# Z projections in front of the running places, and state products grouped by form, in a fused embed, state-space and experts kernel

## The reference

```python
h = concatenate([tok(A, B, x, log_dt), softmax(table)[x_txt]], axis=1)     # 16 x 192 x 512
zxbcdt = layernorm(h) @ W_in.T                      # z 1024, x 1024, B 64, C 64, dt 16
xBC = silu(causal_conv4(xBC)); dt = softplus(dt + dt_bias)
state = state * exp(dt * A) + dt * B * x            # per head (16 heads of 64 channels)
y = state . C + D * x                               # for every token
y = rmsnorm(y * silu(z)) * norm_w
h = h + y @ W_out.T
h = h + experts(layernorm(h))                       # router: top 8 of 32 experts, rerouted by similarity
```

## Time and profile before

| | |
|---|---|
| median of 3 runs | 1762.59 us (1762.48 to 1763.11) |
| profiled execution, its own time | 1780.81 us |
| its span in the trace | 1779.1 us |
| mean granted TensorE clock | 0.917 of full |
| TensorE matmul busy | 1574.6 us, 89% |
| VectorE busy | 971.2 us, 55% |
| ScalarE busy | 730.3 us, 41% |
| GpSimd busy | 781.5 us, 44% |
| matmuls of line 1213 (state products, main) | 512 records, 84.7 us |
| matmuls of line 1216 (state products, tail) | 512 records, 49.0 us |

### The profile page before, as it was taken

How to read it: one execution, slowest core, us unless ns; L and a number is a source line. 1 busy time by engine, 2 the same in 40 slices (tenths; PEclk the granted TensorE clock), 3 DMA queues, 4 the chain that set the end, 5 groups by cost and what they waited for, 6 DMA issues and landing times. The chain is left out here.

```text
span 1779.1 us, 31373 instructions
## 1 busy us (share of the span) xinstructions
PE 1574.6 (89%) x9263; PEld 1146.1 (64%) x9264; DVE 971.2 (55%) x2325; ACT 730.3 (41%) x1592; POOL 781.5 (44%) x638
## 2 busy tenths in 40 slices
PE   7999999997599999999999670099999999999996
PEld 7999999975477576675766340066655666666564
DVE  5555554523768998889789545034333343433443
ACT  2525253522776765857658100033333333333332
POOL 4230300011042357677675567545544555555554
PEclk9999999988799998998899575599999999999999
DMA  7210000003355352443423110167767777777665
GB/s 267 77 60 1 13 1 13 1 18 134 114 152 143 93 153 77 134 130 93 151 64 90 27 37 2 60 181 190 159 154 188 162 181 167 169 183 182 162 114 92
DMA packets 97703, 195.20 MB, mean 110 GB/s; under 512 B 38391, under 2 KB 46879, under 8 KB 92880
## 3 DMA queue, kind: packets, MB, share of 16 engines
q0 software_dynamic: 36992, 88.26, 23.1%
q1 hardware_dynamic: 60624, 105.78, 19.5%
HBM read 144.15 MB, written 49.84 MB: 109 GB/s over the span
## 5 line engine op out<-in xcount | busy, mean ns | idle before, releaser
L1888 PE MATMUL moe_ps_gu<-moe_wgu,moe_xt 128*128 x960 | 331.9, 489 | 0.0
L1746 POOL DMA_INDIRECT out_h<-moe_yy,moe_idx_s x121 | 190.9, 1578 | 256.2 <-DVE moe_idx_s L1808 117.4
L1016 POOL DMA_INDIRECT scratch_slots<-lay_toki,lay_slot x192 | 219.9, 1145 | 59.0 <-issue 58.1
L1888 PEld LDWEIGHTS moe_ps_gu<-moe_wgu,moe_xt 128*128 128x128 f32 x960 | 173.7, 191 | 96.6 <-issue 1.2
L1785 ACT ACTIVATE moe_sl<-moe_ps_gu 128x192 f32<-128x192 f32 x120 | 39.7, 331 | 365.7 <-PE moe_ps_gu L1888 336.2
L1411 DVE SCALAR_TENSOR_TENSOR lay_xa<-lay_ring,head_cw,lay_xa 128x378 f32<-128x378 f32 (+5 forms) x240 | 141.9, 609 | 54.4 <-ACT lay_xa L1068 46.0
L1197 PE MATMUL lay_ring<-lay_xnt,win_sb 128*128 128x128 f32 (+2 forms) x1152 | 167.6, 292 | 4.3 <-DVE lay_xa L1411 2.0
L1281 PE MATMUL lay_ring<-head_wout,lay_yb 128*128 128x512 f32 x384 | 170.1, 597 | 0.0
L1197 PEld LDWEIGHTS lay_ring<-lay_xnt,win_sb 128*128 128x128 f32 (+2 forms) x1152 | 150.6, 200 | 10.5 <-issue 3.8
L1740 POOL DMA_INDIRECT moe_xg<-scratch_xg,moe_idx_g x123 | 131.4, 1069 | 47.5 <-issue 28.7
L247 POOL TENSOR_TENSOR tok_vv<-tok_w 128x512 f32<-128x512 f32 x16 | 16.6, 1040 | 259.7 <-ACT tok_w L449 225.5
(11 more groups left out here) (290 smaller groups left out, 2961.5 us busy)
## 6 DMA issues: line engine op xcount, KB each, us to landing
lay_m<-scratch_cum SPq DMA_DIRECT2D x16, 1536.0 KB
moe_wgu<-in_wgu SPq DMA_DIRECT2D x32, 768.0 KB
moe_wd<-in_wd SPq DMA_DIRECT2D x32, 384.0 KB
out_h<-lay_hres SPq DMA_DIRECT2D x48, 128.0 KB
scratch_xg<-lay_x SPq DMA_DIRECT2D x48, 128.0 KB
win_sb<-in_win SPq DMA_DIRECT2D x1, 4384.0 KB, 16.3
tok_u_raw<-in_tok_u SPq DMA_DIRECT2D x16, 256.0 KB, 4.5
tok_v_raw<-in_tok_v SPq DMA_DIRECT2D x16, 256.0 KB, 5.1
```

The costliest lines, as they stand in the source:

```text
L1016: pool.indirect_dma_start(out=a["slots"], out_offset=bass.IndirectOffsetOnAxis(ap=slot[:, j, k:k + 1], axis=0), in_=toki[:, j:j + 1], in_o ...
L1746: pool.indirect_dma_start(out=a["out"], out_offset=bass.IndirectOffsetOnAxis(ap=idx_s[n][:, 0:1], axis=0), in_=yy[n][:], in_offset=None, b ...
L1888: last = mm(ps_gu[b][:], xt[b][:, t], wgu[:, bass.ds(r * KD + t, 1)].rearrange("p o n -> p (o n)"), start=t == 0, stop=t == KD - 1)
```

## The change

The change does two things, in TensorE's list and in the order of the ring.

First, four z projections (PL_BEHIND = 4) come in front of the running places of pair w, and the other four behind them. In the ring the places' use moves behind z 3 as well, for every pair.

Second, state_products is called as often as before and still makes four heads a call, but of two channel tiles whose results lie in two banks: the four mains follow one another, then the four tails. Two calls together fill the two banks; both banks are taken at the first of the two calls, and both are given to VectorE at the end of the second.

```diff
+PL_BEHIND = 4
...
         if 0 <= i < PAIRS:
             order += [("y", i, k) for k in range(N_Y)]
+        if n < PAIRS:
+            order += [(c, n, k) for c, k in XZ_ORDER[:PL_BEHIND]]
         if 0 <= i - 2 < PAIRS - 2:
             order.append(("pl", i - 2, 0))
         if n < PAIRS:
-            order += [(c, n, k) for c, k in XZ_ORDER]
+            order += [(c, n, k) for c, k in XZ_ORDER[PL_BEHIND:]]
...
-                def state_products(i, b, m2):
-                    out = take_bank("y", i, b * 4 + m2)
-                    for m in (2 * m2, 2 * m2 + 1):
-                        c0 = (m % 2) * SEQ
-
-
+                def state_products(i, b, u):
+
+                    places = [("y", i, b * 4 + u // 2 * 2 + q) for q in range(2)]
+                    outs = [take_bank(*use) if u % 2 == 0 else bank(*use) for use in places]
+                    c0 = u % 2 * SEQ
+                    tiles = [(out, 2 * (u // 2 * 2 + q) + u % 2) for q, out in enumerate(outs)]
+
+
+                    for out, m in tiles:
                         for h in (2 * m, 2 * m + 1):
                             p0 = (h % 2) * HP
                             mm(out[p0:p0 + HP, c0:c0 + SEQ], xdt[:, b, h * HP:(h + 1) * HP], m0[:, b, h], start=True, stop=False)
+                    for out, m in tiles:
                         for h in (2 * m, 2 * m + 1):
                             p0 = (h % 2) * HP
                             last = mm(out[p0:p0 + HP, c0 + S0:c0 + SEQ], xdt[b * S1:(b + 1) * S1, 2, h * HP:(h + 1) * HP],
                                       m1[b * S1:(b + 1) * S1, h], start=False, stop=True)
-                    last.then_inc(ring_pe, 1)
+                        if u % 2:
+                            last.then_inc(ring_pe, 1)
...
-                    if listed_late(w):
-                        places(w)
+                    for k in range(MI):
+                        if k == PL_BEHIND and listed_late(w):
+                            places(w)
+                        if pairs(n):
+                            project(n, "z", k, COL_Z + k * P, P)
                     if pairs(n):
-                        for k in range(MI):
-                            project(n, "z", k, COL_Z + k * P, P)
                         pe.wait_ge(td_in_done, n + 1)
```

## The result

| | before | changed |
|---|---|---|
| median of nine runs | 1763.91 us (1762.48 to 1774.91) | 1779.22 us (1768.20 to 1785.89) |
| ratio of the runs | | 1.0057, 95% interval 1.0036 to 1.0078 |
| profiled execution, its own time | 1780.81 us | 1770.55 us |
| span; mean granted clock | 1779.1 us; 0.917 | 1768.8 us; 0.928 |

What follows compares the result with a forecast made beforehand. Within a pair, TensorE gains are lost where it waits for VectorE, ScalarE or GpSimd. Pair terms summed to +2.2 us on 1762.59 us, giving 1764.8 us, no change; the range was 1755 to 1774 us.

Steps and rivals of the forecast that it cites:

- A call saves 0.31 us: State products on TensorE: fewer changes of form take a call from 1.475 to 1.163 us at full clock.
- rival (a): State products: weights of the next head are not loaded ahead, so a call saves nothing; +11.4, about 1774 us; chance 0.08.
- Batch 1 starts at 8.33: Products of batch 1 wait for VectorE's skip, starting at t = 8.33 instead of 5.92, with TensorE idle for 3.6 us.
- z 4 waits for ScalarE, no wait before the places, x 7 held by the convolutions in pair 4: z 4 starts at 27.0 after SiLU of z 0; the mask wait (3.10 us in pair 2) disappears; x 7 stays at 40.94.
- Falling in batch 1 it is absorbed by the wait for the gate: Half clock after the new idle time, if in batch 1's products, costs nothing; at z 4 it costs 2.6 us a pair.
- Rival (b): New idle time brings half clock, harmful at z 4: +10 us in four pairs, about 1775 us; in two, 1770; chance 0.27.
- Pairs 3 and 5, +2.3 us each: TensorE is late on half clock, so VectorE waits for the later places and x 7 is delayed: +2.3 us each.
- rival (c): Denser products and z filling the mask wait make the clock fall less: -6 to -9, 1755 to 1759 us; chance 0.18.
- Pair 0, +0.7: At half clock batch 1 starts at 486.7 instead of 484.41; four calls give back 1.6 us: +0.7 us.
- pair 1, +1.1: z 4 cannot start before z 5 did, so everything behind is one z later: +1.1 us.
- pair 2, -1.0: The wait for the mask is filled, so x 7 may start at 648.9 instead of 649.93: -1.0 us.
- Pair 7, -3.2: No B/C projections in front, so the skip of y 0 is early and all eight calls save 0.4 us: -3.2 us.

Runs made afterwards that it cites:

- the grouping alone: Kernel before with state products grouped over two banks and no z moved in front of the places: 1772.36 us, ratio 1.0024.
- The wait alone: Kernel before, products and places unchanged, but TensorE takes both y banks at the first call of each two: 1814.94 us, ratio 1.0144.
- set 3: On one chip beside the kernel before (1786.19 us): the change again (1799.71 us, 1.0078) and three kernels with VectorE's skip of y 0 between the matrix halves.
- the skip alone: Kernel before with only VectorE's skip of y 0 moved between the two halves of the masked matrices: 1783.81 us, ratio 0.9997.
- the skip between: The whole change, with VectorE's skip of y 0 moved between the two halves of the masked matrices: 1768.88 us, ratio 1.0010.
- the z alone: Kernel before with four z in front of the places and state products as before: 1769.57 us, ratio 1.0013.
- the first two calls as before: The whole change, but calls 1 and 2 of batch 1 are the old ones of one bank each: 1774.92 us, ratio 1.0057.
- The kernel that beats the change: Kernel before with products of four heads grouped, old z order, skip of y 0 between the halves of the masked matrices: 1779.03 us, ratio 0.9955.

## Where the prediction was right and where it was wrong

- **A call saves 0.31 us: right.** It saves 0.295. The weights of the next head are loaded ahead within one form, and rival (a) is out. The Trainium skill, "TensorE: Matmul & The Clock Gate", Part 3, has weight loads overlap only at another row group; by that a call would have saved nothing, and the trace has 1.18 us for 1.475.
- **Batch 1 starts at 8.33: right**, 8.34, with the wait where it was put. **z 4 waits for ScalarE, no wait before the places, x 7 held by the convolutions in pair 4: right.** Pair 4 took 71.6 us where 72.4 was forecast. The z in front of the places alone measured +0.13%, not told from zero.
- **"Falling in batch 1 it is absorbed by the wait for the gate": this is the step that failed.** The half clock was not a case beside the sum but belonged in it: in the profile of the change a stretch of it begins in every pair from 1 to 6, right behind the idle time. And it was sized from the earlier trace rows at 3.4 us lost, which is 6.8 us at half clock. The runs have 3.4 us at half clock in some pairs, which the gate does absorb (71.6 us), and 20.5 us, some 10 us lost, in others, which it does not (78.1 us in pair 2, and 75.5 and 75.7 in pairs 1 and 5 of the grouping alone). In pair 1 even 3.4 us of it went with 67.8 us against 65.9. The wait alone, without the shorter products, cost 25 us, where the forecast priced its 2.4 us a pair as hidden or as 1 us. Rival (b) had the mechanism, and its 1775 us are 12 us of loss where 10 were measured; but it put the harm at z 4, and the rows have it in batch 1. That the size fits is in part luck: it was added up from another place, and the half clock does not account for the whole loss (the table of set 3). The earlier trace rows had shown what 3.10 us of idle time did, and the sum put a longer one into six pairs at no price for the clock.
- **Pairs 3 and 5, +2.3 us each: wrong, and read from a poor witness.** The half clock of pair 5 before began behind stalls that another execution doesn't have. Without them the changed kernel took 72.9 and 71.6 us there; with them 76.2 and 74.9, against 78.1 and 78.4 of the kernel with the skip alone. So behind stalls the change has less half clock there, as rival (c) said, and gains 1.9 and 3.5 us; it doesn't make up for the others. Without stalls there is no profile of the kernel before to compare with.
- **Pair 0, +0.7, pair 1, +1.1, pair 2, -1.0:** set 3 has pair 0 at -0.5, pair 1 at +1.9 and pair 2 at +6.1 us against the skip alone. Pair 2 is the mis-sized term of the most weight.
- **Pair 7, -3.2: not steady.** In the three profiles without stalls that group all of its calls (the change, the grouping alone, the skip between) it took 59.3, 58.5 and 55.1 us, not grouped (the z alone) 63.8. In the profiles with stalls it took 63.9 to 67.8 us grouped and 64.4 to 67.5 not grouped. Grouping it alone gave 0.9984, not told from 1.
- **What stays open.** That taking two banks at once costs by the wait it brings is shown: the wait alone measures 1.0144. How the loss of the whole change divides between half clock, plain delay and the z is not. The kernel that beats the change differs from it in two edits, the skip and the order of the z. The z's own measured price (at most 0.28% by its interval) is less than a quarter of the 20.7 us (1.2%), but that the two don't add to more together was not run in one set. What the stalls of "issue" wait for, and why executions of one kernel differ in them, is open too. Grouping all four heads within one bank, which would need no second bank, was not tried.

## What to carry to other kernels

An idle gap in front of TensorE's products is not priced by its length alone, but also by what the clock may do behind it: here 2.36 us of waiting cost 12.1 us in a pair. When an edit makes one step take two buffers at once, look for the step whose second buffer comes free last, and bring forward the single instruction that frees it; here that, together with the old order of the z, turned a loss of 0.8% into a gain of 0.45% on the same chip. And before terms are read from one profile, hold its own time against the timed runs: a profile 17 us above the median may hold stalls that the median run doesn't.

## What the chip showed that was not expected

- TensorE's clock fell to 1.2 GHz behind very short idle times in the loose old products: 0.95 and 0.28 us (pairs 3 to 6 of the kernel with the first two calls as before), 0.50 and 0.44 us (pair 5 before). It does not always: in pairs 1 and 2 of the same kernel it stayed up through the products behind the same 0.95 and 0.28 us, and behind a single 0.62 or 0.47 us (pairs 4 and 6 before) it did not fall until t = 17.6 and 20.2. The Trainium skill, "TensorE: Matmul & The Clock Gate", section "HAM oscillation", names idle gaps between bursts as what brings the lower clock round after round. The trace agrees in the pairs where it fell, with gaps down to a microsecond; the page's own example has longer ones, waits for a DMA.
- Once it was down from the first half of the products on, it came back after 3.4 or 6.8 us, or only with the z, 17 to 24 us later. With the products as before and a wait of 1.10 to 2.37 us in front of them it was the long one in all three pairs that had the wait (1, 2 and 6 of the kernel with the wait alone); with grouped products it was either, for the same instructions.
- VectorE's two small adds of the counts took 3.82 us beside GpSimd's gate and 1.69 us when the change had moved them to 783.47 us, 1.4 us before its end.
